# Moving the weight loads, the page stores and a gather in the attention part of a fused layer kernel

## The reference, cut to what matters

```python
q = jnp.einsum('bsd,ed->bse', x, Wq).reshape(bsz, seqlen, HQ, D)
k = jnp.einsum('bsd,ed->bse', x, Wk).reshape(bsz, seqlen, HK, D)
v = jnp.einsum('bsd,ed->bse', x, Wv).reshape(bsz, seqlen, HK, D)
q = _rope(_rmsnorm(q, q_norm_w), pos)
k = _rope(_rmsnorm(k, k_norm_w), pos)
kc = k_cache[block_table].reshape(bsz, L, HK, D)
vc = v_cache[block_table].reshape(bsz, L, HK, D)
k_all = jnp.concatenate([kc, k], axis=1)
v_all = jnp.concatenate([vc, v], axis=1)
scores = jnp.einsum('bqhd,bkhd->bhqk', q, repeat(k_all)) * SCALE
probs = jax.nn.softmax(jnp.where(valid, scores, -1e+30), axis=-1)
o = jnp.einsum('bhqk,bkhd->bqhd', probs, repeat(v_all))
x = x + jnp.einsum('bse,de->bsd', o.reshape(bsz, seqlen, HQ * D), Wo)
```

## Time and profile before

| what | value |
|---|---|
| median of three executions | 1353.04 us |
| profiled execution | 1358.97 us, span 1356.4 us |
| PE busy | 1293.1 us (95%) |
| DVE busy | 1015.4 us (75%) |
| POOL busy | 926.2 us (68%) |
| ACT busy | 840.8 us (62%) |
| DMA moved | 265.86 MB, mean 196 GB/s |

### The profile page before, as it was taken

How to read it: one execution, slowest core, us unless ns; L and a number is a source line. 1 busy time by engine, 2 the same in 40 slices (tenths; PEclk the granted TensorE clock), 3 DMA queues, 4 the chain that set the end, 5 groups by cost and what they waited for, 6 DMA issues and landing times.

```text
span 1356.4 us, 25339 instructions
## 1 busy us (share of the span) xinstructions
PE 1293.1 (95%) x7068; PEld 1120.5 (83%) x7068; DVE 1015.4 (75%) x2054; ACT 840.8 (62%) x2217; POOL 926.2 (68%) x1173
## 2 busy tenths in 40 slices
PE   9888999999999998999999989998999999999999
PEld 8766788888888887888888878887888778888887
DVE  6766778678877887787778867877878887748545
ACT  7555576566665766676657666656766775535444
POOL 7776788778787887788678877877887842305111
PEclk9988899999999999999999999999999999999999
DMA  5588658956895699569856976696675454354542
GB/s 200 187 230 274 179 156 253 291 125 173 256 299 134 165 266 271 140 180 275 241 155 173 302 205 177 187 296 193 184 205 156 132 178 152 124 178 144 186 140 77
DMA packets 260052, 265.86 MB, mean 196 GB/s; under 512 B 139776, under 2 KB 211072, under 8 KB 249216
## 3 DMA queue, kind: packets, MB, share of 16 engines
q1 hardware_dynamic: 254208, 228.77, 58.7%
q0 software_dynamic: 5760, 36.18, 8.0%
HBM read 182.57 MB, written 82.31 MB: 195 GB/s over the span
## 4 chain that ended last, share of the span: by engine, by line
PE 56%; DMA 13%; DVE 9%; POOL 9%; issue 7%; ACT 3%; SPq 2%; POOLq 0%; ACTq 0%; DVEq 0%
PE ps L65 17%; PE ps L66 16%; PE ps L67 16%; DMA at_pT_raw<-turned_rows 5%; POOL at_probs L607 4%; DMA turned_rows<-at_turned 4%; DMA kT_pages<-shared 3%; PE ps L1329 3%; DVE at_pT_lo L1000 2%; ACT at_probs L789 2%; DVE at_turned L1087 2%; SPq L402 2%; DVE ds_lo L1000 1%; DVE at_probs L1052 1%; ACT at_pT_hi L737 1%
## 5 line engine op out<-in xcount | busy, mean ns | idle before, releaser
L789 ACT ACTIVATE at_probs<-at_probs,at_neg_max 128x640 f32<-128x640 f32 x256 | 210.2, 823 | 133.9 <-DVE at_neg_max L1052 133.9
L607 POOL TENSOR_SCALAR at_probs<-at_probs,at_row_inv 128x640 f32<-128x640 f32 x256 | 210.6, 833 | 93.2 <-DVE at_row_inv L1062 81.6
L1052 DVE CUSTOM_DVE_ANT_0 at_probs<-ps,at_mask,at_inv_rms 128x640 f32<-128x640 f32 x256 | 223.1, 880 | 16.6 <-PE ps L67 13.9
L65 PE MATMUL ps<-ds_hi,x_hi 128*128 128x512 f32 (+1 forms) x564 | 196.0, 347 | 3.6 <-DVE x_lo L1000 2.4
L67 PE MATMUL ps<-ds_hi,x_lo 128*128 128x512 f32 (+1 forms) x564 | 194.2, 344 | 0.0
L737 ACT ACTIVATE at_pT_hi<-ps 128x512 fp32r<-128x512 f32 x196 | 111.4, 603 | 88.6 <-PE ps L1329 84.2
L65 PE MATMUL ps<-at_kT_hi,ds_lo 128*128 128x320 f32 x512 | 159.9, 312 | 3.9 <-DVE at_pT_lo L1000 1.4
L65 PE MATMUL ps<-at_pT_hi,at_v_hi 128*128 128x512 f32 x320 | 130.9, 409 | 32.6 <-DVE at_pT_lo L1000 26.0
L66 PE MATMUL ps<-at_kT_lo,ds_lo 128*128 128x320 f32 x512 | 158.3, 309 | 0.0
L67 PE MATMUL ps<-at_kT_hi,ds_lo 128*128 128x320 f32 x512 | 158.3, 309 | 0.0
L1087 DVE STREAM_TRANSPOSE at_turned<-at_probs 128x768 f32<-128x768 f32 x62 | 60.7, 978 | 113.3 <-POOL at_probs L607 113.3
(11 more groups left out here) (226 smaller groups left out, 3647.4 us busy)
## 6 DMA issues: line engine op xcount, KB each, us to landing
turned_rows<-at_turned SPq DMA_DIRECT2D x62, 512.0 KB
at_pT_raw<-turned_rows SPq DMA_DIRECT2D x248, 128.0 KB
kT_pages<-shared SPq DMA_DIRECT2D x16, 1024.0 KB, 5.6
q_rows<-at_q_turned_rows SPq DMA_DIRECT2D x248, 64.0 KB, 2.4
at_qT_raw<-q_rows SPq DMA_DIRECT2D x62, 256.0 KB, 3.2
kv_raw<-kT_pages SPq DMA_DIRECT2D x60, 256.0 KB, 4.0
v_pages<-shared SPq DMA_DIRECT2D x14, 1024.0 KB, 5.7
kv_raw<-v_pages SPq DMA_DIRECT2D x56, 256.0 KB, 3.4
```

Source lines behind the costliest of these rows:

```text
L65: pe.matmul(out, l_hi, r_hi, start=first, stop=False)
L607: pool.tensor_scalar(probs[:, h, :], probs[:, h, :], row_inv[:, h:h + 1], 1.0, ALU.mult, ALU.mult).then_inc(probs_done, 1)
L789: act.activation(probs[:, h, :], probs[:, h, :], ACT.Exp, bias=neg_max[:, h:h + 1], scale=-1.0, accum_out=row_sum[:, h:h + 1]).then_inc(ex ...
L1052: dve.tensor_tensor_reduce(out=probs[:, h, :], in0=slot(h), in1=mask[:, b, :], scale=inv_rms[b % 2][:, h:h + 1], scalar=3.0e38, op0=ALU.ad ...
```

## The change

- SP, weights: `load_qkv` is split into `load_wkv` and `load_wq`. In a looped group the key and value weights are loaded at the end of round 0 and the query weights in round 1 behind the reads of the turned rows; in group 0 both are loaded at the start of rounds 0 and 1. Query and output weights now count on one semaphore (`staging_loaded`), key and value weights on another.
- SP, pages: in the looped groups `store_pages` stands behind the reads of the turned rows. In group 0 the second store of first keys moves from the end of round 1 to round 2 behind the read of the queries, and one load of keys moves behind the reads of the turned rows.
- POOL: chunk 3 of the query weights counts on its own semaphore (`wq_pool_done`) and no longer waits for DVE's chunks. The gather stands behind `cached_values`. In round 0 of group 0 `rotate_q` stands ahead of `rotate_k` and the two chunks of output weights.
- ACT and DVE, group 0: the high part of the tokens stands ahead of the output weights; DVE turns the queries of round 0 one `mask_and_max` earlier.

```diff
+        def wq_by_dve(g, c):
+            return c + 1 if by_row(g) else g * (DC - 1) + min(c, DC - 2) + 2
...
+            def load_wq(g):
+                sp.dma_start(wq_raw[:], wq[bass.ds(g, 1)].rearrange("o p c d -> p (o c) d")).then_inc(staging_loaded, 16)
+
+            def load_wkv(g):
+                sp.dma_start(wkv_raw[:], wkv[bass.ds(g, 1)].rearrange("o p c d -> p (o c) d")).then_inc(wkv_loaded, 16)
...
-                    if not last and b == 4:
-                        wait_apart(sp, wo_pool_done, g * 2 + 2, passed)
-                        wait_apart(sp, wo_dve_done, g * 2 + 2, passed)
-                        wait_apart(sp, wkv_done, g * KV_GROUPS + KV_GROUPS, passed)
-                        load_qkv(g + 1)
-                    if by_row(g2) and b2 >= KEY_ROWS:
+                    if by_row(g) and b == 0:
+                        sp.wait_ge(wkv_done, KV_GROUPS)
+                        load_wkv(1)
+                    if by_row(g) and b == 1:
+                        sp.wait_ge(wo_pool_done, 2)
+                        sp.wait_ge(wo_dve_done, 2)
+                        load_wq(1)
+                    if by_row(g) and b == KEY_ROWS - 2:
+                        store_first_keys(1)
+                    if by_row(g2) and b2 > KEY_ROWS:
...
-                    if not by_row(g) and not last and 2 <= b < 6:
-                        store_pages(g, b - 2)
...
                     if by_moves(g, b):
                         read_turned(g, b)
+                    if not by_row(g) and not last and b == 1:
+                        wait_apart(sp, wo_pool_done, g * 2 + 2, passed)
+                        wait_apart(sp, wo_dve_done, g * 2 + 2, passed)
+                        load_wq(g + 1)
+                    if not by_row(g) and not last and 2 <= b < 6:
+                        store_pages(g, b - 2)
...
             def wq_group(g, n):
                 wait_apart(pool, wq_hi_done, g * DC + n + 1, passed)
-                wait_apart(pool, wq_done, g * DC + n, passed)
-                pool.tensor_tensor(wqT_lo[:, n, :], wq_raw[:, n, :], wqT_hi[:, n, :].bitcast(F32), ALU.subtract).then_inc(wq_done, 1)
+                pool.tensor_tensor(wqT_lo[:, n, :], wq_raw[:, n, :], wqT_hi[:, n, :].bitcast(F32), ALU.subtract).then_inc(wq_pool_done, 1)
...
+                    rotate_q(g2, b2)
+                    if started:
+                        key_scale(g2, b2)
+                        cached_values(g1, b1)
+                        stage()
                     else:
                         rotate_k(g2, b2)
                         wo_group(g, 0)
                         wo_group(g, 1)
-                    rotate_q(g2, b2)
-                    if started:
-                        key_scale(g2, b2)
-                        stage()
-                        cached_values(g1, b1)
...
+                    if by_row(g) and b < B - 3:
+                        tokens(b + 3)
                     if b == 0:
                         for n in range(WO_GROUPS):
                             wo_group(g, n)
-                    if by_row(g) and b < B - 3:
-                        tokens(b + 3)
...
                     mask_and_max(g1, b1, 0)
+                    if not started:
+                        spread_queries(g2, b2)
                     mask_and_max(g1, b1, 1)
                     if started:
                         turn_k(g2, b2)
-                    else:
-                        spread_queries(g2, b2)
```

More of the change, by code:

```diff
@@ L196, in attention @@
         ident_step = sem("ident_step")
-        wq_half_loaded = [sem(f"wq_half_loaded{j}") for j in range(2)]
+        wq_half_loaded = sem("wq_half_loaded")
         table_step = sem("table_step")
@@ L205, in attention @@
         xT_done = sem("xT_done")
-        wqkv_loaded = sem("wqkv_loaded")
-        wo_loaded = sem("wo_loaded")
+        staging_loaded = sem("staging_loaded")
+        wkv_loaded = sem("wkv_loaded")
         wq_hi_done = sem("wq_hi_done")
@@ L210, in attention @@
         wq_done = sem("wq_done")
+        wq_pool_done = sem("wq_pool_done")
         wkv_done = sem("wkv_done")
@@ L452, in group @@
                         read_turned(g, b)
+                    if not by_row(g) and not last and b == 1:
[4 more added lines that the diff above has]
+                        store_pages(g, b - 2)
+                    if by_row(g2) and b2 == KEY_ROWS:
+                        sp.wait_ge(kv_stored, STAGED_FIRST)
+                        sp.wait_ge(kc_done, b + 1)
+                        load_keys(g2, b2)
                     if last and b == 1:
@@ L467, in group @@
                     if by_row(g):
-                        if b < 2:
-                            store_first_keys(b)
-                        elif b < 6:
+                        if b == 0:
+                            store_first_keys(0)
+                        elif 2 <= b < 6:
                             store_pages(g, b - 2)
+                    elif not last and b == 0:
+                        wait_apart(sp, wkv_done, g * KV_GROUPS + KV_GROUPS, passed)
+                        load_wkv(g + 1)
                     if last and b in (0, 2, 4, 5):
@@ L744, in qkv_group @@
                 if first and n < DC:
-                    hi(out, src, wq_half_loaded[n // 2], 16, wq_hi_done)
+                    hi(out, src, (wq_half_loaded, staging_loaded)[n // 2], 16, wq_hi_done)
                 else:
-                    hi(out, src, wqkv_loaded, g * 32 + 16, wq_hi_done if n < DC else wkv_hi_done)
+                    hi(out, src, *((staging_loaded, g * 32 + 16, wq_hi_done) if n < DC else (wkv_loaded, g * 16 + 16, wkv_hi_done)))
             def wo_group(g, n):
@@ L1284, in project_q @@
                     if b == 0:
-                        pe.wait_ge(wq_done, g * DC + c + 1)
+                        if by_row(g) or c < DC - 1:
+                            pe.wait_ge(wq_done, wq_by_dve(g, c))
+                        else:
+                            pe.wait_ge(wq_pool_done, g)
                     ins = three_pass(pe, bank(project_bank(g, b)), xT_hi[:, c, at], xT_lo[:, c, at], wqT_hi[:, c, :], wqT_lo[:, c, :], c == 0, c == DC - 1)
```

14 lines of the change are left out of this document (6 added, 8 removed).

## The result

| what | before | after |
|---|---|---|
| median | 1353.04 us | 1345.58 us (11 runs each) |
| profiled execution | 1358.97 us, span 1356.4 | 1345.42 us, span 1343.4 |
| mean granted clock | 0.986 | 0.995 |

The ratio is 0.9944, 95% interval [0.9925, 0.9964]: 7.5 us faster, where 26 were forecast. The two profiled executions lie 13.6 apart.

A forecast was written before the change was run, and what follows sets the result against it. PE's own work bounds the rounds (15.28 us without waits), leaving 36 us in group 0 and 50 in the loops to win. Group 0 -22 and loops -4 make -26, from the median 1353.0 to 1327 us, range 1309 to 1349.

The forecast's parts named there:

- The ruler: Rounds where POOL is late: the round lasts the larger of 15.28 us and first normalise + 5.97 us.
- Pages behind the reads: Looped rounds 2 to 4: later page stores delay POOL's gather and first normalise, costing 5.2 us a group.
- case A: Rival, chance 0.17: page stores behind the reads find DMA engines free, land quicker, 10 us more won: 1317 us.
- POOL's own semaphore: Looped round 5: POOL's chunk 3 no longer waits for DVE's chunk 2, gaining 2.5 us a group, bounds 0 and 3.1.
- Weights out of round 4: Looped round 4: PE's wait for moved probabilities and its clock loss go, gaining 3.4 us a group, bounds 2.4 and 4.7.
- I charge 0, at most 0.5 a group: Looped round 1: query weights meet the queries' write and read, which have slack; cost 0, at most 0.5 us a group.
- group 0's sum: All rounds of group 0 together: shorter waits and less clock loss win 22 us, bounds 12 and 28.
- Rounds 1 and 3 get 0.5 each: Group 0, rounds 1 and 3: each 0.5 us longer for the query weights and the later gather.
- (0,5): -2.5 by the own semaphore: Group 0, round 5: 3.5 us above 15.28, shortened by 2.5 us through POOL's chunk having its own semaphore.
- Case B: Rival, chance 0.13: three looped rounds in a row with short waits lower PE's clock, 11 us lost: 1338 us.
- Case D: Rival, chance 0.10: rounds (0,2) and (0,4) keep their 5 us waits, group 0 gives 9 us: 1340 us.
- Case C: Rival, looped rounds 2 to 4: gather's wait for stores landing in 6.57 us loses 28: 1355; chance 0.10, slower 0.08.

The follow-up runs named there:

- the second experiment: Changed kernel with group 0's page stores one round later, directly behind the turned write: 1340.09 us, ratio 0.9902 to the kernel before.
- the fourth experiment: Changed kernel with both weight loads back in round 4, ahead of the load of keys: 1362.63 us, ratio 1.0067 to the kernel before.
- the fifth experiment: Changed kernel with POOL's gather of pages back ahead of cached_values: 1376.32 us, ratio 1.0164 to the kernel before.
- the first experiment: Changed kernel with the page stores of groups 1 to 6 back between write and reads of the turned rows: 1310.52 us, ratio 0.9683 to the kernel before.

## Why the prediction was wrong in size

**The sign and the mechanisms in the loops were right.** *The ruler* held to 0.1 us. *Pages behind the reads*: forecast 5.2 a group. Without the edit rounds 2 to 5 take 15.3, 15.3, 15.3 and 16.0, with it 16.0, 18.0, 16.7 and 16.8: 5.6, and 6.4 with (1,2). The stores landed in 4.4 to 4.7 us and not in the 5.0 I took, so case A had the landing right. Its 1317 was wrong all the same: round 5, which starts late behind the three, keeps 0.8 that I had not charged to them. *POOL's own semaphore*: forecast 2.5, measured 2.9 in round 5 alone. *Weights out of round 4*: forecast 3.4. Only 12.3 / 6 = 2.1 are seen with the stores late; but with the stores early these two and the gather's place together give (783.7 - 744.2) / 6 = 6.6 a group, forecast 5.9 for the two. The net of the loops is 1.3 won and not 4. The missing part lies in round 2, where the query weights and the gather stretched the queries' write of (1,1) to 8.57 us. "I charge 0, at most 0.5 a group" was near it in the sum, which is 2.5 to 3.7 us in all, 0.4 to 0.6 a group, but charging 0 was not. That (1,2) alone took 4.2 us of it is one execution's.

**The step that failed is group 0's sum**, -22 forecast and -12.5 measured, and in it two entries. "Rounds 1 and 3 get 0.5 each": round 3 got 4.6. I took out the wait of (0,2) by looking at what stood ahead of its turned write, and put the read of the queries at nothing. SP's page store at the end of (0,2) waits for the gather, and the queries' read stands behind it in SP's list. While PE lost 4.9 us in (0,2), that read left 8.3 us ahead of its round; now it leaves 1.5 ahead, takes 5.3 beside the store, and PE waits 3.27 for the queries in place of the moved probabilities. (0,4) has the same new wait of 3.17, so of its -6.8 it got -5.2. The second experiment shows it: with the store behind the read, rounds 3 to 6 are 5.6 shorter. There the read still leaves only 1.9 us ahead of (0,3) but takes 2.9; no run issues it earlier by itself, so what the late start alone costs is not shown. "(0,5): -2.5 by the own semaphore": it got 2.4 longer. The removed wait did exist there (its return makes the round 24.7). In its place stand the queries again (1.83 of wait), a lower clock, and POOL's work of 19 us, which the waits of (0,4) had covered. The last of these is argued from POOL's busy time and from the 17.4 us of the fourth experiment; why nearly the same work takes 19.5 to 22.2 us in different versions is not settled.

**Case B was right in the wrong place.** In after's loops, where PE's waits were 1.1 us at most and once 1.6, no window shows a clock below 1.00; in group 0, behind waits of 3.27, 3.17 and 1.83, the granted clock was 0.92, 0.92 and 0.84 and took 6.6 us, about what the forecast had booked as won in (0,4) and (0,6), 3.3 + 3.1. The rows draw no sharp line: in the second experiment, with the same loops, (4,4) and (5,4) ran at 0.90 with one wait of 0.96 us in each. The Trainium skill (TensorE: Matmul & The Clock Gate, "A second HAM failure mode: psum-queue depth-cycling") has frequent short idles swing the clock. The rows of the fifth experiment (waits in pieces of 0.2 to 1.6 us, 0.96 and 0.86) agree with it, the looped rounds of after don't, and the drops of (0,3) and (0,4) each follow one wait of about 3.2 us, which is another case.

**Case D** (group 0 gives 9, 1340) came nearest by its number, and by luck: (0,2) did lose its wait, and the new wait of (0,3) came with the page store and the queries' read, not with the query weights. Group 0 gave 12.5 and not 9, and the rest of its distance lay in the loops and the base. **Case C** needed landings of over 6.4 us; no row of after's chain in the loops has more than 4.7.

**The base was wrong too.** "The terms are the same in them": the profiled execution of before was 5.9 above the median, and I subtracted the full sum from the median. The profiled executions differ by 13.6, the medians by 7.5. So 6 of the 18.6 us of error lie in the base, 9.5 in group 0 and 2.7 in the loops. The clock tells most of it. Of 51 further executions of before, the 16 with a mean granted clock of 0.986 or 0.987 have a median of 1358.5 us, the 19 at 0.990 or 0.991 one of 1353.5; the profiled one had 0.986. So it held more clock loss than most, and the forecast took the loss in its rows as there to be won. Which stretch is shorter in a median execution stays open, since no trace of one is there.

## What to carry to other kernels

When a wait is taken out of one round, the next round starts earlier, and transfers that the wait had given time to land are now late: go through every transfer that the following round needs, before the whole wait, and the clock loss that hung on it, are booked as won. The releaser that a row of PE names may itself have waited: follow it to the transfer. A round can't get shorter than the busy time of its fullest engine, so read that column first, of the round before it too. A large transfer whose buffer gates the next gather did best in this kernel between a write and the reads that must wait for that write anyway; there it was free, and about 5 us later in the round it cost 6.4 us a group. And a forecast from one profiled execution holds for that execution: how far it lies from the median is an error of its own.

## What the runs showed of the hardware

The write of the turned rows (0.5 MB) took 2.86 us with no store ahead of it and 7.43 with a 1 MB store and two loads issued within the 2 us ahead of it. The DMA engines were busy for 0.97 of those 7.43 us, though for only 0.78 of the whole round. The read of the queries took 4.7 to 5.7 us with that store just ahead of it and 2.9 to 3.0 with the store behind it. The Trainium skill (DMA: Bandwidth & Descriptors, "Issuing engines are not separate DMA queues") has transfers of all issuers run on the same 16 engines and interleave; the rows agree, and show the price for the ones that come behind. In the loops of the first experiment, with the store behind the write and ahead of the reads, the DMA share is 0.97 and PE is busy all the time: the mean share says little of what a transfer's place costs.
